# A graph layer with experts between its edges: end of a tile tested at every edge slot, one slot retaken, 32 tiles computed ahead

## What is computed

```
x = x + segment_sum((layernorm(x) @ W)[src] * weight, dst) + b
xf = layernorm(x)
# one routing for all rows, from the mean row: softmax, capacity, top 2 of 8
y = sum over the 2 chosen experts of gate * (gelu(xf @ W1[e] + b1[e]) @ W2[e] + b2[e])
x = x + layernorm(y + xf) * gamma + beta
```

## Time and profile before

| | |
|---|---|
| median of three runs | 3268.88 us (3258.56 to 3274.06) |
| span of the profiled execution, from its first to its last instruction | 2384.3 us |
| busy: PE matmul | 2211.0 us |
| busy: PE weight load | 1730.4 us |
| busy: DVE | 1052.3 us |
| busy: ScalarE | 1193.0 us |
| busy: POOL | 1598.6 us |
| gathers, line 588 | 1563, about 946 ns each |
| edge matmul instructions, line 1451 | 3126 |
| mean granted TensorE clock | 0.984 |

### The profile page before, as it was taken

How to read it: one execution, slowest core, us unless ns; L and a number is a source line. 1 busy time by engine, 2 the same in 40 slices (tenths; PEclk the granted TensorE clock), 3 DMA queues, 4 the chain that set the end, 5 groups by cost and what they waited for, 6 DMA issues and landing times. The chain is left out here.

```text
span 2384.3 us, 41652 instructions
## 1 busy us (share of the span) xinstructions
PE 2211.0 (93%) x9949; PEld 1730.4 (73%) x9950; DVE 1052.3 (44%) x2924; ACT 1193.0 (50%) x3203; POOL 1598.6 (67%) x1626
## 2 busy tenths in 40 slices
PE   2488999899999999999999999999998999999998
PEld 1366777676776777777777777777776777999997
DVE  7883223232232223232322323232222235899999
ACT  3577667665665555545534343322324116656654
POOL 6777777777777777777777777777777772242341
PEclk9999999999999999999999999999999999999999
DMA  9955667665656665566656655656565554333422
GB/s 371 333 170 156 203 203 241 186 188 180 184 183 182 179 176 175 178 185 192 186 176 189 189 172 188 182 169 190 179 193 165 183 162 135 101 113 110 134 92 68
DMA packets 226740, 425.79 MB, mean 179 GB/s; under 512 B 36675, under 2 KB 134774, under 8 KB 226600
## 3 DMA queue, kind: packets, MB, share of 16 engines
q0 software_dynamic: 75008, 204.90, 28.6%
q1 hardware_dynamic: 151160, 217.12, 27.9%
q10 hardware_dynamic: 432, 2.40, 0.3%
HBM read 341.53 MB, written 82.75 MB: 178 GB/s over the span
## 5 line engine op out<-in xcount | busy, mean ns | idle before, releaser
L588 POOL DMA_INDIRECT G<-xr_d,SRC x1467 | 1391.7, 949 | 446.9 <-issue 302.5
L1087 DVE TENSOR_SCALAR OH<-CST,DL,WR 128x128 f32<-128x128 f32 x1563 | 569.2, 373 | 1271.0 <-PE ps L1451 1140.1
L1451 PE MATMUL ps<-G,OH 128*128 x3126 | 739.5, 389 | 78.7 <-DVE OH L1087 58.7
L1451 PEld LDWEIGHTS ps<-G,OH 128*128 128x128 f32 x3126 | 596.7, 194 | 224.8 <-issue 143.3
L1434 PE MATMUL ps<-W2u,H 128*128 128x256 f32 x1920 | 430.6, 382 | 6.8 <-issue 6.0
L1423 PE MATMUL ps<-YU,W1u 128*128 128x512 f32 (+1 forms) x1024 | 426.4, 569 | 9.7 <-ACT H L783 8.5
L1434 PEld LDWEIGHTS ps<-W2u,H 128*128 128x128 f32 x1920 | 362.7, 191 | 69.4 <-issue 20.8
L1423 PEld LDWEIGHTS ps<-YU,W1u 128*128 128x128 f32 x1024 | 195.1, 191 | 206.3 <-issue 184.9
L791 ACT ACTIVATE YE<-ps 128x512 f32<-128x512 f32 (+1 forms) x128 | 72.6, 569 | 442.2 <-PE ps L1434 442.1
L783 ACT ACTIVATE H<-ps,b1a 128x512 f32<-128x512 f32 (+1 forms) x256 | 168.6, 661 | 226.1 <-PE ps L1423 225.8
L612 POOL TENSOR_TENSOR ZR<-ZV,mhalf 128x4 f32<-128x4 f32 (+1 forms) x23 | 31.4, 1366 | 218.0 <-DVE ZV L1259 218.0
(11 more groups left out here) (221 smaller groups left out, 2395.8 us busy)
## 6 DMA issues: line engine op xcount, KB each, us to landing
W1u<-in_W SPq DMA_DIRECT2D x64, 512.0 KB
W2u<-in_W SPq DMA_DIRECT2D x64, 512.0 KB
y_d<-YE SPq DMA_DIRECT2D x56, 512.0 KB, 5.4
G<-xr_d,SRC POOLq DMA_INDIRECT x1467
x_d<-X SPq DMA_DIRECT2D x98, 128.0 KB
yt_d<-YT SPq DMA_DIRECT2D x98, 128.0 KB, 3.3
XR<-in_x SPq DMA_DIRECT2D x97, 128.0 KB, 3.2
XL<-x_d SPq DMA_DIRECT2D x24, 512.0 KB, 4.7
```

The lines of the kernel that those rows point to most:

```text
L588: e.indirect_dma_start(out=G[0:rows(s), held(s), :], out_offset=None, in_=x if s < FRESH else xr_d, in_offset=bass.IndirectOffsetOnAxis(ap ...
L1087: e.tensor_scalar(OH[:, s % OHR, :], iota, DL[:, s:s + 1], WR[:, s + 1:s + 2], ALU.is_equal, ALU.mult).then_inc(s_oh, 1)
L1451: e.matmul(ps[:, 0, 0:D], OH[:, r, :], Gf[:, bass.ds(g + r * D, D)], start=False, stop=True, skip_group_check=True).then_inc(s_main, 1)
```

## The change

THR holds the exact slot of a tile's end, `event` stands behind every slot, not behind every other one, and `begin` multiplies only that slot again, so OHX and what leads to it have one matrix in place of two. The group of two tiles moves from the front to place eight: the first eight groups all have four tiles (32 tiles ahead), the group of two is the first of those computed later, and `by_size` is gone. `root` runs one section later and stands between AT and XH. The planner's weights for placing units change a little.

```diff
-SMALL = 2
-NG = (NT - SMALL + GT - 1) // GT + 1
 AHEAD = 8
+SMALL = NT - AHEAD * GT - (NT - AHEAD * GT) // GT * GT
+SIZES = [GT] * AHEAD + [SMALL] + [GT] * ((NT - AHEAD * GT) // GT)
...
-    room = [max(0.0, 0.75 * slots[t] - 3.5) * most[t] if t >= 14 else 0.0 for t in range(NT)]
+    room = [max(0.0, 0.8 * slots[t] - 3.0) * most[t] if t >= 15 else 0.0 for t in range(NT)]
...
-        root = together.get(x1)
+        root = together.get(copied[v - 3]) if v >= 3 else None
+        waiting += root or []
         xh = waiting.pop(0) if waiting else None
-        waiting += root or []
...
                 if s >= HELD:
-                    e.wait_ge(s_main, s - RING + 3)
+                    e.wait_ge(s_main, s - RING + 2)
...
             def copy(v, t):
...
-                for k in range(2):
-                    e.activation(OHX[:, k, :], OHT[:, 1, k, :], ACT.Copy, scale=WR[:, bass.ds(odd + k, 1)]).then_inc(s_ohx, 1)
+                e.activation(OHX[:, :], OHT[:, 1, :], ACT.Copy, scale=WR[:, bass.ds(cut + 1, 1)]).then_inc(s_ohx, 1)
...
                     e.sem_inc(s_at, 1)
+                if s["root"] is not None:
+                    root(s["root"])
                 if s["xh"] is not None:
...
-                if s["root"] is not None:
-                    root(s["root"])
...
-            e.tensor_scalar(THR[0:1, 0:NT - 1], FROW[0:1, 1:NT], 1, None, ALU.bitwise_or).then_inc(s_tab, 1)
+            e.tensor_copy(THR[0:1, 0:NT - 1], FROW[0:1, 1:NT]).then_inc(s_tab, 1)
...
-                e.matmul(ps[:, 0, 0:D], OHX[:, 0, :], Gf[:, bass.ds(g, D)], start=True, stop=False, skip_group_check=True)
-                e.matmul(ps[:, 0, 0:D], OHX[:, 1, :], Gf[:, bass.ds(g + D, D)], start=False, stop=True, skip_group_check=True).then_inc(s_begin, 1)
+                e.matmul(ps[:, 0, 0:D], OHX[:, :], Gf[:, bass.ds(g, D)], start=True, stop=True, skip_group_check=True).then_inc(s_begin, 1)
...
-                            by_size(unit_down)
+                            unit_down(e.snap(u_r, min_val=0, max_val=UNITS - 1))
...
                     edge(g, r)
-                    if r % 2 == 1:
-                        event(a, r, g)
+                    event(a, r, g)
...
-        "iota_e": (np.arange(NE) // 2 * 2).astype(np.float32)[None], "evt": evt,
+        "iota_e": np.arange(NE, dtype=np.float32)[None], "evt": evt,
```

More of the change, by code:

```diff
@@ L23 @@
 XG = (NT + GT - 1) // GT
-SMALL = 2
-NG = (NT - SMALL + GT - 1) // GT + 1
 AHEAD = 8
+SMALL = NT - AHEAD * GT - (NT - AHEAD * GT) // GT * GT
+SIZES = [GT] * AHEAD + [SMALL] + [GT] * ((NT - AHEAD * GT) // GT)
+STARTS = [sum(SIZES[:g]) for g in range(len(SIZES))]
+NG = len(SIZES)
 UNITS = AHEAD * E
@@ L43, in group, with place_in @@
 def group(t):
-    return 0 if t < SMALL else (t - SMALL) // GT + 1
+    return max(g for g in range(NG) if STARTS[g] <= t)
 def tiles(g):
-    a = SMALL + (g - 1) * GT
-    return range(a, min(a + GT, NT)) if g else range(SMALL)
+    return range(STARTS[g], STARTS[g] + SIZES[g])
+def place_in(t):
+    return t - STARTS[group(t)]
 def part(t):
-    return slice((t - SMALL) % GT, (t - SMALL) % GT + 1)
-def place_in(t):
-    return t - tiles(group(t))[0]
+    return slice(place_in(t), place_in(t) + 1)
 def slot(t):
@@ L87, in events @@
     most = [0.75 if t == NT - 1 else 1.0 for t in range(NT)]
-    room = [max(0.0, 0.75 * slots[t] - 3.5) * most[t] if t >= 14 else 0.0 for t in range(NT)]
-    size = [len(tiles(k // E)) / GT for k in range(UNITS)] + [1.0]
+    room = [max(0.0, 0.8 * slots[t] - 3.0) * most[t] if t >= 15 else 0.0 for t in range(NT)]
     free, u, out = 0.0, 0, []
     for t in range(NT):
-        free += room[t] * sum(size) / sum(room)
+        free += room[t] * (UNITS + 1) / sum(room)
         n = 0
-        while u + n <= UNITS and (free >= size[u + n] / 2 or t == NT - 1):
-            free -= size[u + n]
+        while u + n <= UNITS and (free >= 0.5 or t == NT - 1):
+            free -= 1.0
             n += 1
@@ L477, in _ @@
                             e.wait_ge(yt_st[t % 4], 16 * (t // 4 + 1))
-                        e.dma_start(YL0[:, :, :], yt_d[post[0], :, :, :]).then_inc(yl_in[0], 16)
+                        w = len(tiles(post[0])) * P
+                        e.dma_start(YL0[:, :, 0:w], yt_d[post[0], :, :, 0:w]).then_inc(yl_in[0], 16)
                     if n == GT + 2:
@@ L1422, in unit_up, with unit_down @@
                     for c in range(2):
-                        ins = e.matmul(ps[:, UP[i % 2], 0:m * P], W1u[:, c, i * P:(i + 1) * P], YU[:, c, 0:m * P], start=(c == 0), stop=(c == 1))
+                        ins = e.matmul(ps[:, UP[i % 2], :], W1u[:, c, i * P:(i + 1) * P], YU[:, c, :], start=(c == 0), stop=(c == 1))
                     ins.then_inc(s_up, 1)
-            def unit_down(u, m):
+            def unit_down(u):
                 e.wait_ge(w2_in, u * 16 + 16)
@@ L1430, in unit_down @@
                     e.wait_ge(s_ye, u * 2 + (p + 1))
-                    for h in range(m // 2):
-                        j = m - 1 - (m // 2 * p + h)
+                    for h in range(GT // 2):
+                        j = GT - 1 - (GT // 2 * p + h)
                         for i in range(4):
@@ L1468, in event @@
                         with e.If(now < DOWNS):
-                            by_size(unit_up)
+                            unit_up(e.snap(u_r, min_val=0, max_val=UNITS - 1))
                     with e.Else():
@@ L1523, in keep_warm @@
                 for _ in range(n):
-                    e.matmul(ps[:, 7, :], ones_r[:, :], YTh[:, 0, 0, :], start=True, stop=True, skip_group_check=True)
+                    e.matmul(ps[:, 7, :].rearrange("p (c n) -> p c n", c=2), ones_r[:, :], YTh[:, 0, :, 0:SMALL * P], start=True, stop=True, skip_group_check=True)
             t = NT - 1
             e.wait_ge(s_ye, 2 * UNITS + 2)
-            e.wait_ge(s_yth, 1)
+            e.wait_ge(s_yth, 2)
             keep_warm(6)
```

35 lines of the change are left out of this document (14 added, 21 removed).

## The result

| | before, same chip and session | changed |
|---|---|---|
| median | 3263.72 us (3254.8 to 3274.06, 4 runs) | 3306.36 us (3304.15 to 3311.15, 4 runs) |
| ratio | | 1.0136, 95% interval 1.0108 to 1.0164 |
| span of its profiled execution | 3227.5 us (`b_again`, below) | 3303.5 us |

What follows compares the result with a forecast made beforehand. POOL's gathers set stage one's end, with PE and its sequencer almost level. Tests +181, retake -42, deviations -18, tiles +52 make +173; less margin 30 and stage two's 9, +134: 3403 us, range 3256 to 3480 (8 in 10).

Steps and rivals of the forecast that it cites:

- The base: Whole run: changes summed on the 2384.3 us span, added to the 3268.88 us median, the 884.6 us between taken as unchanged.
- Price and place of the tests: PE's sequencer in the edge laps: 780 more tests at 0.36 us each, 281 us, net +181 after cover.
- a lap of 4.9 us: PE's sequencer, eight edges: a lap grows from 3.45 to 4.9 us with eight tests, against 3.45 us of matmuls.
- cover of 100: PE's sequencer behind expert units: its lead hides 100 us of the added tests, at most 147.
- margin of 30: PE against POOL's gathers in stage one: between 12 and 45 us of PE time to spare, taken as 30.
- One slot retaken, -42: PE at 97 tile ends: two matmul instructions fewer at each save 42 us, bounds -34 and -76.
- Inverse deviations, -18: ScalarE's sections: the move shortens PE's AS waits, part returning as later waits; between -36 and +12, taken -18 us.
- 32 tiles ahead: +52 in stage one, -9 in stage two: Eight expert units grow to four tiles, +52 us of PE; one stage-two group shrinks to two tiles, -9 us.
- The total: Whole kernel: +173 us of PE in stage one, +143 after the margin, +134 after stage two; 3403 us.
- the signs: Profile after: about 1730 test rows, no more than some 30 instruction packets, stage one ending about 2120, AS waits below 20 us.
- POOL's waits: POOL between gathers in stage one: idle over 0.30 us, waiting for PE's edge matmuls.
- the sequencer's rule: PE's sequencer: other instructions are queued while a control instruction executes, so tests would be free; tests staying covered had chance 0.18.

Runs made afterwards that it cites:

- b_again: The kernel before, unchanged, profiled once more: 3229.34 us, span 3227.5 us.
- experiment 1: The kernel before, unchanged, profiled again to see whether the 884 us lie outside the span: 3229.34 us, span 3227.5 us.
- b_thin_2: The kernel before with each gather from slot 96 on fetching 16 of 128 rows: 3293.81 us in its one run, against 3237.47 of before.

## Why the prediction was wrong

Step by step, in its order.

- **The base failed.** "The 884.6 us between them lie before the first and behind the last instruction ... I take them as unchanged ..." All but 1.8 us of a run lie inside its span (experiment 1). The sum was made on a short execution and added to the median of long ones. A span 884 us under the runs should have told me that it was not one of them; the prediction made no rival of that. The line in the section on the profile before, that this time isn't in the trace, is wrong for the same reason.
- **Price and place of the tests: right, on the trace from which they came.** 0.36 us a test (0.35 measured); a lap of 4.9 us (4.83); cover of 100 and margin of 30: 281 - 100 - 30 = 151 us, and 154 were measured at the short level. The price was read; that the sum comes so near is partly luck, as the cover was a choice between 60 and 147. At the long level 36.
- **One slot retaken, -42: absent.** The matmul put back costs 18 to 23 us, but the part as a whole changes the time from 2551.41 to 2553.14 us beside the tests.
- **Inverse deviations, -18: no gain.** 0 on before (-2 to +3), 8 to 10 us dearer in the changed kernel. I had the preload, XH and YT behind them as the price, with +12 as the bound; the bound held, the value taken did not.
- **32 tiles ahead: +52 in stage one, -9 in stage two: too large, and absent.** It costs 8 us alone, where a margin is left, and 11 beside the tests. My reading is that there the array has slack in every test-bound lap, and each longer unit gives the sequencer more lead for the next tests: the two work against each other, and a sum of separate terms counts the same time twice. It fits the two numbers; no run isolates it.
- **The total** at the level of the trace: 134 predicted, 174 measured, 1.0725. The parts measured one upon the other, tests, tiles, exact slot, inverse deviations, are 154 + 11 + 0 + 10 us; predicted they were 151 + 43 - 42 - 18. The 32 us too much for the tiles hid part of the 70 by which the last two terms were too low, which is luck. At the level of the times: 134 predicted, 43 measured. There the step that failed is the margin, "PE has a margin of between 12 and 45 us", taken as 30. PE stood idle for 784 us in `b_again`, not 173 as in the trace that I read, and 400 for 103 (58.7 + 35.7 + 8.5) of them are put down to one-hots, H and AS. Of the tests' 154 us, 118 went into that idle time, and of the change's 174, 131. Only the direction, slower, came out at both levels.

Of the signs: 1732 test rows, a lap of 4.8 us and 28 packets came as said, and so did "issue" and POOL's waits at the short level; stage one ended at 2156 (2120 said) at the short level; AS waits under 20 us came at the short level (13.5) but not at the long (53.6); stage two did not get 9 us shorter (406 for 407). By the sequencer's rule in the Trainium skill, "Advanced Engine Details and Errata", Sequencer Loop, that I weighed, the tests would have been free; runs at both levels speak against it for this loop.

**What stays open.** What makes signals late at the long level. It is not the fetched bytes (`b_thin_2`, one run). It isn't a difference of code, as the same kernel has both levels. Nor, it seems, is it the chip: the record gives one chip number for a session of each level, twice (1 and 10). Whether the recording of the profile has a part in it, as the fewer records might suggest, no run tested. Whether added matmuls are absorbed there as tests are wasn't seen. Why the exact slot brings PE more waiting for one-hots, and why the moved deviations cost 8 to 10 us beside the tests, stay open too. And none of the kernels beat the one before.

## What to carry to other kernels

Compare the profiled span with the runs' times before anything is costed: here they differed by 1.8 us where profile and times were of one kind and by 884 where not, and PE's idle time was 784 us in one and 173 in the other. A sequencer test on a register costs about 0.35 us on PE; beside two matmuls of 0.22 us a slot, one test to every slot makes the sequencer slower than the array (a lap of 4.83 us against 3.48), and only time in which the array runs behind its sequencer, or waits anyway, hides it. Count copies of unrolled code before adding to a loop: the loop of 744 pairs was slower by a factor of 3.1, not by per cents, and the instruction queue's packets show it at a glance. And measure parts one upon the other: the parts' gains beside the tests were not those that they had in the sum.

## What the runs showed of the hardware

- Before takes 2388 or about 3225 to 3265 us, by session and not by run. 793 of the 843 us between the spans are in the edge stage, where PE's register moves of 37 ns reach 711 ns and engines that had waited 3 to 11 us start within 0.31 us of each other.

```profile
L1460 PEldq MOVE  x950: 3/37/711, 134.9 to 2818.5; - x190
```

- At that level added tests are partly free: they cost 23% (36 of 154 us) and 62% (419 of 680 us) of what they cost at the other.
- A loop fetched anew in each of 195 laps took 10 instruction packets a lap and 2.6 us a packet, and the mean granted clock fell to 0.626 as PE stood waiting, from 0.985.
